# Loading the first images and the embedding weights ahead of the constants, and embedding the first group ahead of the weight products

## The reference

```
patches = X.reshape(B, C, 8, 28, 8, 28).transpose(0, 2, 4, 1, 3, 5).reshape(B, 64, 2352)
tokens  = einsum('bpi,hi->bph', patches, W) + b
tokens  = concatenate([cls, tokens], axis=1) * pos_embed
h       = concatenate([tokens, txt], axis=1)
h       = h + attn(layernorm(h), wq, wk, wv, w1, w2, ...)      # complex weights per head, real part taken
h       = h + ffn(layernorm(h), Wq, ..., gate_W, W1, W2, ...)  # attention, then 8 experts, top 1
```

## Time and profile before

| what | value |
|---|---|
| median of three runs | 1433.87 us (1432.84 to 1434.1) |
| the profiled execution, its own time | 1432.25 us |
| its span in the profile | 1430.4 us |
| PE busy | 1341.3 us, 94% |
| DVE, ACT, POOL busy | 71%, 51%, 29% |
| mean granted TensorE clock | 0.974 |
| first weight product, start | 9.41 us |
| first embedding, start | 16.44 us |
| first tokens made by DVE | 27.35 us |

### The profile page before, as it was taken

The page is one execution under the profiler, slowest core; times in us unless marked ns, Lnnn a source line. Parts: engine busy times, 40 slices in busy tenths (PEclk is TensorE's granted clock), DMA queues, the critical chain, the costliest instruction groups (busy, mean ns, idle before and its releaser), DMA issues. The chain is left out here.

```text
span 1430.4 us, 40339 instructions
## 1 busy us (share of the span) xinstructions
PE 1341.3 (94%) x14876; PEld 984.3 (69%) x14877; DVE 1008.9 (71%) x2308; ACT 723.4 (51%) x1630; POOL 411.4 (29%) x268
## 2 busy tenths in 40 slices
PE   6889999999999999999999999999999861999996
PEld 5457666666666666666666666666665550999996
DVE  1477777777777777777777777777778643566664
ACT  2135555555555555555555555555555451556654
POOL 0000222222222222222222222222222224466665
PEclk9999999999999999999999999999999895999999
DMA  7522322232222222322233333333310002333331
GB/s 296 216 73 72 83 83 82 83 83 83 83 83 83 83 83 82 83 83 83 83 86 89 93 88 86 88 95 84 85 42 15 18 14 54 104 104 102 102 100 53
DMA packets 94839, 124.57 MB, mean 87 GB/s; under 512 B 56587, under 2 KB 77117, under 8 KB 94176
## 3 DMA queue, kind: packets, MB, share of 16 engines
q1 hardware_dynamic: 38112, 102.47, 22.7%
q0 software_dynamic: 56576, 19.93, 6.7%
HBM read 101.27 MB, written 20.82 MB: 85 GB/s over the span
## 5 line engine op out<-in xcount | busy, mean ns | idle before, releaser
L1126 POOL DMA_INDIRECT expert_rows<-row_sb,placei x128 | 275.7, 2154 | 618.9 <-DVE z L922 566.9
L359 PE MATMUL bank_emb<-x_sb,wtok 128*128 128x256 f32 (+1 forms) x1216 | 323.5, 393 | 4.4 <-DMA x_sb<-in_x_main 3.4
L359 PEld LDWEIGHTS bank_emb<-x_sb,wtok 128*128 128x128 f32 (+1 forms) x1216 | 220.8, 191 | 104.0 <-issue 50.8
L862 DVE TENSOR_TENSOR sm<-bank_s,con 97x776 f32<-97x776 f32 x256 | 240.1, 959 | 26.1 <-PE bank_s L413 13.8
L876 DVE TENSOR_REDUCE mx<-bank_s 97x8 f32<-97x776 f32 x128 | 120.4, 961 | 57.9 <-PE bank_s L479 57.7
L1297 POOL DMA_INDIRECT out_tokens<-yo,tok x104 | 126.1, 1213 | 90.9 <-issue 55.0
L413 PE MATMUL bank_s<-qm,xn 32*97 32x452 f32 x1024 | 133.3, 583 | 4.3 <-DVE prob L881 2.2
L881 DVE TENSOR_TENSOR prob<-bank_s,mx 97x776 f32<-97x776 f32 x128 | 120.7, 964 | 3.3
L731 ACT ACTIVATE prob<-prob 97x776 f32<-97x776 f32 x128 | 108.4, 847 | 26.5 <-DVE prob L881 26.5
L1227 PE MATMUL bank_s<-w2e,hid 128*128 x832 | 109.7, 275 | 0.0
L869 DVE COPY vp<-bank_s 97x128 f32<-97x128 f32 x256 | 70.3, 286 | 55.6 <-PE bank_s L413 55.4
(11 more groups left out here) (181 smaller groups left out, 2330.1 us busy)
## 6 DMA issues: line engine op xcount, KB each, us to landing
x_sb<-in_x_main SPq DMA_DIRECT2D x96, 768.0 KB, 7.2
row<-expert_rows SPq DMA_DIRECT2D x104, 129.0 KB
w1e<-in_exp_w SPq DMA_DIRECT2D x1, 2576.0 KB, 11.7
txt<-in_txt_t SPq DMA_DIRECT2D x32, 64.0 KB, 2.3
w2e<-in_exp_w SPq DMA_DIRECT2D x1, 2048.0 KB, 16.9
expert_rows<-row_sb,placei POOLq DMA_INDIRECT x128, 7.9
out_tokens<-yo,tok POOLq DMA_INDIRECT x104, 2.5
x_sb<-in_x_tail SPq DMA_DIRECT2D x32, 48.0 KB, 2.5
```

Of the source, the lines that this page charges most:

```text
L359: mm = pe.matmul(banks["emb"][:, 0:NPG], wtok[0:k, c, :], x_sb[0:k, c, :], start=(c == 0), stop=(c == KC - 1))
L862: ins = dve.tensor_tensor(sm[:, k % 2, 2 * h:2 * h + 2, :], pair(h), decay, ALU.mult)
L1126: pool.indirect_dma_start(out=rows[:, :], out_offset=bass.IndirectOffsetOnAxis(ap=placei[:, k, c:c + 1], axis=0), in_=row_sb[:, k, c, E:E ...
```

## The change

SP now loads `wtok` and `x_sb` of group 0 in front of everything, in alternating quarters, each quarter of `wtok` with a semaphore of its own. Behind them come `col` and `pos` (semaphore `s_c`), then `wts` and `con` (`s_k`), the text, `tokno` (`s_n`) and `blank`. The wait for `blank` and its store move behind the expert weights. PE embeds group 0 before it makes the weight products, and the steps of its loop leave group 0 out. ACT copies `woc` first instead of last. DVE makes the tokens of group 0 before it waits for the constants.

```
         def _(sp):
-            sp.dma_start(con[:], consts).then_inc(s_c, 16)
-            sp.dma_start(wts[:], weights).then_inc(s_c, 16)
-            sp.dma_start(col[:], columns).then_inc(s_c, 16)
-            sp.dma_start(pos[:], pos_t).then_inc(s_c, 16)
-            sp.dma_start(tokno[:], token_no).then_inc(s_c, 16)
-            sp.dma_start(wtok[:, 0:KC - 1, :], w_main).then_inc(s_w, 16)
-            sp.dma_start(wtok[0:KTAIL, KC - 1, :], w_tail).then_inc(s_w, 16)
...
             for k in range(4):
+                if k < 3:
+                    sp.dma_start(wtok[:, XP[k]:XP[k + 1], :], w_main[:, XP[k]:XP[k + 1], :]).then_inc(s_w[k], 16)
+                else:
+                    sp.dma_start(wtok[0:KTAIL, KC - 1, :], w_tail).then_inc(s_w[k], 16)
                 load_x(0, k)
+            sp.dma_start(col[:], columns).then_inc(s_c, 16)
+            sp.dma_start(pos[:], pos_t).then_inc(s_c, 16)
+            sp.dma_start(wts[:], weights).then_inc(s_k, 16)
+            sp.dma_start(con[:], consts).then_inc(s_k, 16)
...
             load_txt(0)
+            sp.dma_start(tokno[:], token_no).then_inc(s_n, 16)
             sp.dma_start(blank[:], no_token).then_inc(s_blankin, 16)
-            sp.wait_ge(s_blankin, 16)
-            sp.dma_start(rows[E * REG:E * REG + P, :], blank[:]).then_inc(s_blankin, 16)
...
             sp.dma_start(w2e[:], exp_w2).then_inc(s_ew, 16)
+            sp.wait_ge(s_blankin, 16)
+            sp.dma_start(rows[E * REG:E * REG + P, :], blank[:]).then_inc(s_blankin, 16)
...
                     if c in XP:
+                        if g == 0:
+                            pe.wait_ge(s_w[XP.index(c)], 16)
                         pe.wait_ge(s_x[XP.index(c)], (g + 1) * 16)
...
+            def ahead(g, c0, c1):
+                if g:
+                    embed(g, c0, c1)
+
+            embed(0, 0, KC)
+            pe.wait_ge(s_k, 32)
             pe.wait_ge(s_neg, 1)
...
             pe.wait_ge(s_made, 1)
+            pe.wait_ge(s_c, 32)
...
-            pe.wait_ge(s_w, 32)
...
-                at(embed, i + 1, 4, 5)
+                at(ahead, i + 1, 4, 5)
...
         def _(act):
-            act.wait_ge(s_c, 80)
+            act.wait_ge(s_c, 32)
+            act.wait_ge(s_k, 32)
...
             act.wait_ge(s_mm, 1)
+            act.copy(woc[:], banks["s2"][:, 0:P]).then_inc(s_made, 1)
             act.copy(ar[:], banks["s0"][:, 0:P])
...
-            act.copy(woc[:], banks["s2"][:, 0:P]).then_inc(s_made, 1)
...
-            dve.wait_ge(s_c, 80)
+            dve.wait_ge(s_c, 32)
             for k in range(2):
                 dve.tensor_scalar(h0[:, k, :, 0], pos[:, 0:1].to_broadcast([P, G]), column("cls"), None, ALU.mult)
-            dve.tensor_copy(run[:], const("run0")).then_inc(s_zero, 1)
-            dve.wait_ge(s_zero, 1)
-            dve.wait_ge(s_made, 2)
...
+            tokens(0)
+            dve.wait_ge(s_k, 32)
+            dve.tensor_copy(run[:], const("run0")).then_inc(s_zero, 1)
+            dve.wait_ge(s_zero, 1)
+            dve.wait_ge(s_made, 2)
+
+            def tokens_ahead(g):
+                if g:
+                    tokens(g)
```

More of the change, by code:

```diff
@@ L251, in place_tokens @@
         s_xused = [sem(f"x_used{k}") for k in range(4)]
-        s_w, s_c, s_txt, s_blankin = sem("wtok_loaded"), sem("constants_loaded"), sem("txt_loaded"), sem("blank_loaded")
+        s_w = [sem(f"wtok_loaded{k}") for k in range(4)]
+        s_c, s_k, s_n = sem("columns_loaded"), sem("constants_loaded"), sem("token_numbers_loaded")
+        s_txt, s_blankin = sem("txt_loaded"), sem("blank_loaded")
         s_neg, s_mm, s_made, s_zero = sem("neg_wqi_ready"), sem("weight_products"), sem("weights_made"), sem("vector_set_up")
@@ L362, in embed @@
                         mm.then_inc(s_xused[XP.index(c + 1) - 1], 1)
-            pe.wait_ge(s_c, 80)
+            def ahead(g, c0, c1):
[3 more added lines that the diff above has]
+            pe.wait_ge(s_k, 32)
             pe.wait_ge(s_neg, 1)
@@ L563, in _ @@
                 at(b_wo, i - 3)
-                at(embed, i + 1, 4, 5)
+                at(ahead, i + 1, 4, 5)
                 at(b_scores, i - 2, 1)
-                at(embed, i + 1, 5, 9)
+                at(ahead, i + 1, 5, 9)
                 at(c_var, i - 3)
-                at(embed, i + 1, 9, 12)
+                at(ahead, i + 1, 9, 12)
                 at(a_q_real, i)
                 at(a_scores, i - 1, 3)
-                at(embed, i + 1, 12, 15)
+                at(ahead, i + 1, 12, 15)
                 at(a_q_imag, i)
@@ L577, in _ @@
                 at(a_yvar, i - 1)
-                at(embed, i + 1, 15, 18)
+                at(ahead, i + 1, 15, 18)
                 at(c_rows, i - 3, 1)
@@ L586, in _ @@
                 at(b_center, i - 1)
-                at(embed, i + 1, 18, 19)
+                at(ahead, i + 1, 18, 19)
                 at(b_probs_t, i - 2, 0, 2)
@@ L593, in _ @@
                 at(b_probs_t, i - 2, 1, 3)
-                at(embed, i + 2, 0, 1)
+                at(ahead, i + 2, 0, 1)
                 at(b_values, i - 2)
@@ L598, in _ @@
                 at(a_center, i + 1)
-                at(embed, i + 2, 1, 2)
+                at(ahead, i + 2, 1, 2)
                 at(b_scores, i - 1, 0)
@@ L606, in _ @@
                 at(c_rank, i - 3)
-                at(embed, i + 2, 2, 4)
+                at(ahead, i + 2, 2, 4)
                 at(a_scores, i, 2)
@@ L977, in token_numbers @@
                     dve.wait_ge(s_scat[g % ROWS], 16 * G * (g // ROWS))
+                if g == 0:
+                    dve.wait_ge(s_n, 16)
                 dve.tensor_copy(row_sb[:].bitcast(I32)[:, g % ROWS, :, E + 2 * P + 1], tokno[0:S, g * G:(g + 1) * G])
@@ L1046, in _ @@
                 at(top_index, i - 3)
-                at(tokens, i + 1)
+                at(tokens_ahead, i + 1)
                 at(token_numbers, i - 2)
```

## The result

| | before | after |
|---|---|---|
| median | 1436.14 us (17 runs: 1432.23 to 1438.49 and one of 2269.57) | 1430.06 us (17 runs, 1423.75 to 1433.76) |
| profiled execution | 1432.25 us, span 1430.4 | 1433.58 us, span 1431.7 |
| ratio after / before | | 0.9959, 95% interval 0.9948 to 0.9971 |

The change makes the kernel faster by 0.41%: 5.9 us of 1436, with an interval from 4.2 to 7.5 us. The forecast was a gain of 7.4 us and a time of 1426.5, in a range up to 1429.4. The direction is right and the forecast gain lies in the interval, but the time lies 0.7 us above the range. The three runs that stood ahead of the prediction had a median of 1433.87; the 17 runs of the same kernel, these three among them, have one of 1436.14. Single runs far above the rest, such as 2269.57 here, are left out of every ratio.

The account below looks back on a forecast made before the run. PE's gapless middle was taken as the bound, so only an earlier entry counts: 6.3 us at the start plus 1.1 at the wait for group 2's data make 7.4, and 1433.9 - 7.4 = 1426.5 us, range 1423.7 to 1429.4.

Parts of the forecast that it names:

- What bounds the kernel: Middle, 160 to 1060 us: PE busy 900.00 of 900 us, so only its point of entry can give or cost time.
- first term: Start of the kernel: ACT's first square comes at 23.0 instead of 29.36, a gain of 6.3 us.
- The loads: Start, SP's queue: at 381 KB per us the constants land at 17.7 us and `blank` at 18.4.
- The embedding moved ahead: Start, PE: group 0's embedding runs 5.9 to 16.7 us, hidden beside the load of the constants, 1.0 us to spare.
- mark: ACT's first square of the chain, taken as the measure of the start: 29.36 us before, forecast at 23.0.
- Second term: PE's wait for group 2's `x_sb`: PE goes on at 40.0 instead of 47.41, 1.1 us more gain, 7.4 in all.
- B: Start: the clock falls around the products after PE's idle time; gain 5.3 us, time 1428.6; chance 0.20.
- A: PE's wait near 38 to 40 us: the clock stays up through it; gain 8.9 us, time 1425.0; chance 0.18.
- second wait: PE's wait from 44.05 to 47.41 us for group 2's `x_sb`, forecast to become 37.7 to 40.0.
- C: Load queue later than its rate says, delaying group 2's data; at 5% lower rate gain 6.3 us, 1427.6; chance 0.07.
- D: Clock falls at 16.7 us and stays down until group 2; 6.6 us slower, 1440.5; chance 0.05 with anything else eating the gain.

Follow-up runs that it names:

- plain kernels: The kernel before and the changed kernel, without added products in the drain; in the first group 1436.14 and 1430.06 us.
- filled kernel: Kernel before plus products without use in PE's order after the last group's embedding; 1433.54 us (12 runs), ratio 0.9988 to the kernel before without them.
- filled pair: Kernel before and changed kernel, both with products without use added in the drain, on one chip; 1433.54 and 1425.29 us.
- second pair: Kernel before and changed kernel, both unchanged, profiled again on another chip; 1444.92 and 1437.55 us, ratio 0.9950.
- before_again: Kernel before, nothing changed, run for a second profile; 1444.92 us (32 runs).

## Why the prediction was right and wrong, step by step

**What bounds the kernel.** Right for the middle. From the tokens of group 3 to those of group 31 the profiles took 973.9, 974.2, 973.9, 974.0, 974.7 and 974.2 us on the first and the last chip and 982.4 to 984.0 on the others, whatever stood at the start. A shift that enters it leaves it.

**The step that failed: "against the median it is 1433.9 - 7.4 = 1426.5".** The miss is 3.6 us (1430.06 against 1426.5), and 2.3 us of it lie in the number that the gain was taken from. Three runs within 1.3 us of each other were taken as the kernel's level; 17 runs gave 1436.14. The same gain from that level gives 1428.7. "The spread of the runs" was counted as 1 us to either side in the forecast's own range; the changed kernel's 17 runs span 10 us.

**The premise under it: "Whatever PE arrives earlier it keeps, since nothing in that stretch is paced from outside; the expert stage comes after and isn't touched."** This is true for the stretch from 160 to 1060 us that it rested on. It passed over the 140 us behind it, in which PE has gaps and its clock rises and falls. The runs showed that this drain takes 137.5 to 144.6 us in seven profiles of the two plain kernels, the longer the lower the clock granted in it, and that in the first pair it took back all 6.5 us of the start. This is what makes three runs too few. On average no loss in the drain is seen: the ratios 0.9959, 0.9950 and 0.9952 of three groups are gains of 5.9, 7.2 and 6.9 us, beside a mean shift of 6.6 us at the last tokens (5.9 in the three plain pairs). A share of 1 or 2 us wouldn't show in this noise.

**The other 1.3 us are the gain,** 6.1 us between the medians instead of 7.4. The interval of the ratio, 4.2 to 7.5 us, still holds 7.4, so the runs alone don't say that it was too large. The profiles do for the first term, below.

**The loads.** Right within 0.4 us in the profile after. The constants were put at 17.7 and came at 6.62 + 11.5 = 18.1, by this answer on the DMA issues (size, us from issue to landing):

```profile
w2e<-in_exp_w SPq DMA_DIRECT2D x1, 2048.0 KB, 16.2
con<-in_consts SPq DMA_DIRECT2D x1, 1358.0 KB, 11.5
```

`w2e`, issued at 19.65, landed at 35.9; by the rate of the prediction it would have been 36.9. So group 2's data were there ahead of the tokens at 42.1. The landing differs from one execution to the next: in the six profiles with this start, ACT's negation begins at 17.4 to 18.7 us.

The rule of the Trainium skill on batching ("DMA: Bandwidth & Descriptors", section Bandwidth) would have put them 1 us later, an estimate worked out from that page. One profile can't tell 0.4 from 1 us here, but the last of the first loads, `blank`, can: the same 5957 KB lie in front of it and in it in both orders. It landed at 17.9 to 18.8 us, mean 18.4, in the four profiles with `wtok` in one piece that have the kernel before's start, and at 18.0 to 19.3, mean 18.5, in the six with `wtok` in quarters. No run shows the extra 1 us for quarters of 384 KB in a full queue, and the measurement decides.

**The embedding moved ahead.** Right: 6.65 to 16.8 against 5.9 to 16.7, hidden to the last. It started 0.7 us later than worked out, and the 38 records took 10.14 instead of 10.76. In two of the six profiles with this start it ended only 0.7 and 0.4 us ahead of the products, instead of the 1.5 worked out.

**First term, 6.3 us, mark at 23.0: too large.** The products in 1.8 us and ACT's copies as the next bound were right where the clock held: in four profiles the square stands right behind `bo`, at 22.53 to 23.79, each time 5.12 us after the start of ACT's negation (5.3 were worked out). What moves the mark there is the landing of the constants. With the clock down it was 24.66 and 23.98, both 6.4 us after the negation. So the 1.7 us by which the mark of the first profile was late are 0.5 us of the load and 1.3 us of the clock, less the 0.2 us by which the rest was shorter than worked out. The mark of before isn't fixed either: 29.36, 28.52, 28.64, and 30.14 in the filled kernel. Measured, profile against profile on one chip, the term is 4.70, 5.24, 4.66 and 7.36 us (filled pair), against the 6.3 that were forecast.

**Second term, 1.1 us.** The releaser was right: DVE's tokens in all six profiles, the data no longer late. PE went on at 42.19 in the first and at 41.53, 40.05, 39.55, 40.56 and 39.30 in the others, against 40.0. The size wasn't fixed. Group 1's square gained 1.65, 1.32 and 1.32 us more than group 0's in three pairs (the first, the last and the filled one), from the data wait and the clock together. In the second pair it gained 0.67 us less, since the kernel before had no wait for the data to remove.

**Rivals.** B happened in two of six profiles and cost 1.3 us at the mark (6.4 against 5.1 us from the negation), less than its price of 2.1. A happened in the same two and in none of the other four: 43.58 - 42.19 = 1.39 and 42.91 - 41.53 = 1.38 us from the chunk to the square, against 2.52 before and 1.6 to 2.6 in the others. The prediction took A and B as alternatives and gave each a time of its own. In these profiles they came together, so that a part of B's cost came back at the second wait. C and D did not happen.

## What to carry to other kernels

Read every stretch between the place of a change and the end of the span, not only the long gapless one: a stretch in which PE has gaps can differ by more than the whole change from run to run. Two profiles can then contradict two medians, and the shift of one fixed step, followed through the span, tells where they part. A few runs close together are no level to count a small gain from: three spanned 1.3 us, the longer series of the same kernel 6.3. An order of loads and an order of work are one change; each half alone was worth nothing or cost 11 us.

## What the runs showed of the hardware that was not expected

The gapless middle, one order of instructions at a granted clock of 1.00, takes 974 us in the first and the last group and 983 on the two chips between. A round lasts 34.79 us in one and mostly 35.1 in the other. Nearly all of the 0.3 us sit in one place, the products of L427, which come twice in a round. In the first trace (kernel before) both take

```profile
687.04 1.55 PE L427 MATMUL bank_y<-sm,vp 97*32 97x97 f32 x64
```

and in before_again one of the two takes 1.84 to 1.90 us, such as

```profile
723.47 1.85 PE L427 MATMUL bank_y<-sm,vp 97*32 97x97 f32 x64
```

The cause is open. One and the same kernel is 9 us slower on another chip, which is why ratios within a chip are used here throughout.

The column of the granted clock reads 1.00 from 16.4 to 20 us in the profile before, while the same product takes 634 ns there and 379 ns from 20.8 on the earlier trace rows. At the start of a program the durations tell the level and the column doesn't.
